# A Mamba layer between two sparse FFNs on one core: paired scans, the inverse root in PSUM, one gate instruction, moved ticks

## The reference, cut to what matters

```python
def ffn(x):                                    # H = 512, I = 2048
    h = silu(x @ w_gate) * (x @ w_up)
    return keep_two_largest_of_each_four(h) @ w_down
def mam(x):                                    # E = 1024, N = 16, DT = 128
    xn = x * rsqrt(mean(x*x) + EPS) * norm_w
    skip, u = xn @ W_skip.T, silu(conv4(xn @ W_in.T) + conv_b)
    delta = softplus(u @ Wd1.T @ Wd2.T + bd2)
    Bt, Ct = u @ WB.T, u @ WC.T
    h = exp(delta[..., None] * A) * h + (delta * u)[..., None] * Bt    # scan over time
    y = sum_n(h * Ct)
    return ((y + u * W_D) * silu(skip)) @ W_out.T
```

## Time and profile before

| | |
|---|---|
| three runs | 3527.07, 3531.05, 3532.09 us; median 3531.05 |
| the profiled execution | 3525.57 us |
| its span, first to last instruction | 3523.6 us |
| mean granted TensorE clock | 0.987 of 2.4 GHz |
| PE busy | 3339.9 us |
| DVE busy | 3031.5 us |
| POOL busy | 2597.2 us |
| ACT busy | 1999.2 us |
| DMA | 696.44 MB, mean 198 GB/s |

### The profile page before, as it was taken

The page is one execution under the profiler, slowest core; times in us unless marked ns, Lnnn a source line. Parts: engine busy times, 40 slices in busy tenths (PEclk is TensorE's granted clock), DMA queues, the critical chain, the costliest instruction groups (busy, mean ns, idle before and its releaser), DMA issues. The chain is left out here.

```text
span 3523.6 us, 39028 instructions
## 1 busy us (share of the span) xinstructions
PE 3339.9 (95%) x12020; PEld 2110.5 (60%) x12020; DVE 3031.5 (86%) x3597; ACT 1999.2 (57%) x2760; POOL 2597.2 (74%) x1625
## 2 busy tenths in 40 slices
PE   8999999999999999999999999999879889998899
PEld 6775656556655665556655665556545555555467
DVE  5546998789999889989998999999989998999934
ACT  5545656557565664557565674656555665454422
POOL 1315876667878778778787788878989888989913
PEclk9999999999999999999999999999999999999999
DMA  9656566656656566467665675647645565656433
GB/s 362 220 188 195 175 212 219 216 177 222 216 180 227 187 222 227 153 203 230 185 216 185 199 241 179 207 164 237 222 127 206 173 204 211 185 158 196 136 125 117
DMA packets 243469, 696.44 MB, mean 198 GB/s; under 512 B 23536, under 2 KB 23792, under 8 KB 233584
## 3 DMA queue, kind: packets, MB, share of 16 engines
q1 hardware_dynamic: 173632, 559.72, 45.6%
q10 hardware_dynamic: 69632, 134.23, 14.5%
HBM read 619.94 MB, written 76.55 MB: 198 GB/s over the span
## 5 line engine op out<-in xcount | busy, mean ns | idle before, releaser
L1439 POOL TENSOR_TENSOR scan_in<-du,scan_rows 128x512 f32<-128x512 f32 x1024 | 1317.1, 1302 | 628.2 <-DVE decay L1313 537.0
L1313 DVE TENSOR_TENSOR_SCAN decay<-decay,scan_in 128x512 f32<-128x512 f32 x1024 | 1250.8, 1221 | 23.8 <-ACT decay L915 16.5
L1452 POOL TENSOR_TENSOR y<-y,scan_out 128x1024 f32<-128x1024 f32 x512 | 1227.3, 2397 | 0.6 <-DVE scan_out L1323 0.6
L915 ACT ACTIVATE decay<-delta,small 128x512 f32<-128x512 f32 x1024 | 696.9, 688 | 905.4 <-DVE scan_out L1323 897.5
L684 PE MATMUL side<-zhi,wunit 128*128 128x512 f32 x2048 | 905.6, 442 | 40.2 <-DVE zlo L1217 22.5
L774 PE MATMUL side<-h,wdown 128*128 128x512 f32 x1760 | 799.7, 598 | 23.5 <-DVE res_g L1298 12.7
L686 PE MATMUL side<-zhi,wunit 128*128 128x512 f32 x2048 | 814.4, 398 | 0.0
L685 PE MATMUL side<-zlo,wunit 128*128 128x512 f32 x2048 | 812.6, 397 | 0.0
L1323 DVE TENSOR_TENSOR scan_out<-decay,scan_rows 128x512 f32<-128x512 f32 x1024 | 702.6, 686 | 33.3 <-POOL y L1452 8.2
L774 PEld LDWEIGHTS side<-h,wdown 128*128 128x128 f32 x1760 | 333.2, 191 | 391.8 <-issue 347.7
L902 ACT ACT_TABLE_LOAD x407 | 522.2, 1283 | 7.2
(11 more groups left out here) (109 smaller groups left out, 2890.4 us busy)
## 6 DMA issues: line engine op xcount, KB each, us to landing
wunit<-hl_dram SPq DMA_DIRECT2D x480, 512.0 KB, 4.3
scan_rows<-bc_dram ACTq DMA_DIRECT2D x256, 512.0 KB, 5.7
wdown<-down_w_dram SPq DMA_DIRECT2D x256, 256.0 KB, 3.1
wmam<-mam_dram SPq DMA_DIRECT2D x128, 512.0 KB, 4.2
hl_dram<-wunit SPq DMA_DIRECT2D x32, 512.0 KB, 5.2
skip_dram<-skb SPq DMA_DIRECT2D x64, 256.0 KB, 4.6
delta<-skip_dram SPq DMA_DIRECT2D x16, 1024.0 KB, 7.2
wmam<-wout_dram SPq DMA_DIRECT2D x32, 512.0 KB, 4.4
```

The costliest lines, as they stand in the source:

```text
L915: nc.scalar.activation(decay[u % BANKS][:], delta[:, e, :], ACT.Exp, scale=aneg[:, e * N + n:e * N + n + 1]).then_inc(sem["decay_ready"], 1)
L1313: nc.vector.tensor_tensor_scan(decay[u % BANKS][:], decay[u % BANKS][:], db[u % INPUTS][:], 0.0, ALU.mult, ALU.add).then_inc(sem["state_re ...
L1439: nc.gpsimd.tensor_tensor(db[u % INPUTS][:], du[:, e, :], rows[m % ROWS][:, 0, :], ALU.mult).then_inc(sem["input_ready"], 1)
L1452: nc.gpsimd.tensor_tensor(y[:, e:e + 2, :], y[:, e:e + 2, :], scan_out[:, k:k + 2, :], ALU.add).then_inc(sem["sum_ready"], 1)
```

## The change

- DVE's `begin` does two scans and then the two products with C, where a quarter has two units or more.
- The inverse root is written back into the bank that held the variance, and `scale` reads it there (L1203, L1208, L1211). The bank's next owner waits for `scaled`; the planner counts it as taken one tick longer (1.9). The Ln's result stays in SBUF, under a semaphore of its own.
- `gate` is one instruction of 128x2048 in place of four.
- The late deltas go to `STARTS[b] + 7` and `+ 8`. STARTS, and with it all that hangs on it (gates, output projections, some norms and projections), goes from (67, 130, 190, 250, 310, 363, 409, 454, 516) to (67, 130, 191, 250, 312, 359, 409, 454, 515). The pause of seven ticks ahead of product 47 stands ahead of product 45. From its second tick on a half has at least three units done.
- ACT loads a batch's first rows only when its `fold` is past, and takes no unit ahead of time whose delta isn't.
- The planner's costs become tables at the head of the file, with the same values except `var`.

```diff
-PAUSES = {0: 9, 34: 1, 47: 7, 224: 4, 384: 1, 416: 1, 448: 4, 480: 24}
+PAUSES = {0: 9, 34: 1, 45: 7, 224: 4, 384: 1, 416: 1, 448: 4, 480: 24}
...
-STARTS = (67, 130, 190, 250, 310, 363, 409, 454, 516)
+STARTS = (67, 130, 191, 250, 312, 359, 409, 454, 515)
...
-                self.jobs_at[STARTS[b] + 8 + e // 2].append(("dl", b, HE + e))
+                self.jobs_at[STARTS[b] + 7 + e // 2].append(("dl", b, HE + e))
...
-                    upto = start + min(HALF, int(total + 0.5)) if t < end - 1 else start + HALF
+                    upto = start + min(HALF, max(int(total + 0.5), 3 * (t > first))) if t < end - 1 else start + HALF
...
-        read = {"win": 0.2, "down": 0.25, "out": 0.25, "mean": 0.3, "msum": 0.1, "vsum": 0.1, "in": 0.9, "var": 0.9}
+READ = {"win": 0.2, "down": 0.25, "out": 0.25, "mean": 0.3, "msum": 0.1, "vsum": 0.1, "in": 0.9, "var": 1.9, ...
...
         def wait_read(eng, key):
-            eng.wait_ge(sem[f"side_read_{plan.bank_of[key]}"], plan.turn_of[key])
+            if key[0] == "var":
+                eng.wait_ge(sem["scaled"], key[1] + 1)
+            else:
+                eng.wait_ge(sem[f"side_read_{plan.bank_of[key]}"], plan.turn_of[key])
...
                 if u % HE == BANKS - 1:
-                    load_rows(u // HE + 2)
+                    due.append(u // HE + 2)
+                    load_due()
+            def load_due():
+                while due and (due[0] >= B * GROUPS or now[0] > plan.tick_of_job["fold", due[0] // GROUPS] + 1):
+                    load_rows(due.pop(0))
...
                 for u in range(units_done[0], max(units_done[0], min(end + EXP_LEAD, B * UNITS) if end else 0)):
+                    b, half = divmod(u // HALF, 2)
+                    if u >= end and now[0] <= plan.tick_of_job["dl", b, HE * half + HE - 1] + 1:
+                        return
                     unit(u)
...
-                                     scale=1.0 + EPS if double else 1.0).then_inc(read_of(key), 1)
-                wait_read(act, key)
-                nc.scalar.activation(rs, rt, ACT.Exp, scale=-0.5).then_inc(sem["root_ready"], 1)
+                                     scale=1.0 + EPS if double else 1.0).then_inc(sem["log_ready"], 1)
+                act.wait_ge(sem["log_ready"], i + 1)
+                nc.scalar.activation(bank_of(key)[:], rt, ACT.Exp, scale=-0.5).then_inc(sem["root_ready"], 1)
...
                 dve.wait_ge(sem["root_ready"], i + 1)
+                rs = bank_of(("var", i))[:]
...
                 for u in units:
-                    if u > units.start:
+                    second = (u - units.start) % 2
+                    if u > units.start and not second:
                         times_c(u - 1)
                     scan(u)
+                    if second:
+                        times_c(u - 1)
...
-                for k in range(HE):
-                    e = HE * half + k
-                    nc.vector.tensor_tensor(y[:, e, :], y[:, e, :], delta[:, gates_in(b, half).start + k, :],
-                                            ALU.mult).then_inc(sem["gated_ready"], 1)
+                es = halves[half]
+                nc.vector.tensor_tensor(y[:, es, :], y[:, es, :], delta[:, gates_in(b, half), :], ALU.mult).then_inc(sem["gated_ready"], HE)
```

More of the change, by code:

```diff
@@ L85 @@
 SPLIT_AT = 10
+VECTOR = {"mean": 2.3, "down": 0.3, "out": 0.7, "win": 0.6, "in": 1.1, "up": 0.7, "step": 2.9, "low": 2.0, "scale": 3.0, "gate": 2.2, "du": 3.0, "unit": 1.99}
+TENSOR = {"dt": 6.9, "bc": 1.8, "fold": 1.2, "msum": 0.9, "mean": 0.6, "vsum": 0.9, "var": 0.9, "dl": 0.0, "win": 0.7, "down": 3.5, "in": 3.5, "skip": 3.5,
+          "out": 3.5, "product": 2.8}
+READ = {"win": 0.2, "down": 0.25, "out": 0.25, "mean": 0.3, "msum": 0.1, "vsum": 0.1, "in": 0.9, "var": 1.9, "skip": 0.6, "dt": 0.6, "bc": 0.6, "fold": 0.6, "dl": 0.6,
+        "gate": 0.35, "up": 1.35, "first up": 0.55}
 EXP_TABLE, SILU_TABLE, SOFTPLUS_TABLE = "natural_log_exp_and_others", "silu_and_others", "softplus"
@@ L194, in place_units @@
     def place_units(self):
-        vector = {"mean": 2.3, "down": 0.3, "out": 0.7, "win": 0.6, "in": 1.1}
-        tensor = {"dt": 6.9, "bc": 1.8, "fold": 1.2, "msum": 0.9, "mean": 0.6, "vsum": 0.9, "var": 0.9, "dl": 0.0, "win": 0.7}
-        unit = 1.99
+        vector, tensor, unit = VECTOR, TENSOR, VECTOR["unit"]
         def other(tick):
@@ L203, in other @@
             if self.product_at[tick - 1] is not None and is_up(self.product_at[tick - 1]):
[L204 to L207, removed]
+                cost += vector["up"]
+            cost += vector["step"] * (tick - 2 in self.base)
+            cost += vector["low"] * (tick in self.ffn_start or tick in self.split_x_at) + vector["scale"] * (tick in self.scale_at)
+            return cost + vector["gate"] * (tick in self.gate_at) + vector["du"] * (tick in self.du_at)
         def work(tick):
-            return 2.8 * (self.product_at[tick] is not None) + sum(tensor.get(key[0], 3.5) for key in self.jobs_at[tick])
+            return tensor["product"] * (self.product_at[tick] is not None) + sum(tensor[key[0]] for key in self.jobs_at[tick])
         self.units_at = [range(0)] * self.ticks
@@ L242, in place_banks @@
                 if not is_up(n):
-                    free = self.tick_of[4 * (n // 4) + 1] + 1.35
+                    free = self.tick_of[4 * (n // 4) + 1] + 1 + READ["gate"]
                 else:
-                    free = tick + (2.35 if j else 1.55)
+                    free = tick + 1 + READ["up" if j else "first up"]
                 product = [(("product", n), free)]
@@ L248, in place_banks @@
             for key in jobs:
-                side.append((key, tick + 1 + read.get(key[0], 0.6)))
+                side.append((key, tick + 1 + READ[key[0]]))
                 if key[0] == "var" and key[1] in self.alone:
@@ L261, in place_banks @@
                 owner[k] = key
-            if key[0] not in ("awake", "product"):
+            if key[0] not in ("awake", "product", "var"):
                 turns[k] += 1
@@ L362, in build @@
         sq = sb("sq", [P, KD, L])
-        parts, rt, rs = sq[:, 0, :], sq[:, 1, :], sq[:, 2, :]
+        parts, rt = sq[:, 0, :], sq[:, 1, :]
         dts = sb("dts", [P, L])
@@ L382, in build @@
             "member_high_ready", "member_split_ready", "down_high_ready", "down_split_ready",
-            "centred_tile", "squared_tile", "scaled_tile", "squares_ready", "quarter_ready", "root_ready", "scaled", "high_part_ready", "normed_ready",
+            "centred_tile", "squared_tile", "scaled_tile", "squares_ready", "quarter_ready", "log_ready", "root_ready", "scaled", "high_part_ready", "normed_ready",
             "decay_ready", "input_ready", "state_ready", "weighted_ready", "sum_ready",
@@ L916, in unit @@
                 if u % HE == BANKS - 1:
-                    load_rows(u // HE + 2)
+                    due.append(u // HE + 2)
+                    load_due()
+            due, now = [], [0]
+            def load_due():
+                while due and (due[0] >= B * GROUPS or now[0] > plan.tick_of_job["fold", due[0] // GROUPS] + 1):
+                    load_rows(due.pop(0))
             def upto(end):
                 for u in range(units_done[0], max(units_done[0], min(end + EXP_LEAD, B * UNITS) if end else 0)):
+                    b, half = divmod(u // HALF, 2)
+                    if u >= end and now[0] <= plan.tick_of_job["dl", b, HE * half + HE - 1] + 1:
+                        return
                     unit(u)
@@ L1125, in _ @@
                 jobs = plan.jobs_at[tick - 1] if tick else []
+                now[0] = tick
+                load_due()
                 if tick == plan.norm_m[0]:
```

## The result

The changed kernel takes 3488.97 us (median of four runs, 3484.88 to 3490.21) against 3530.86 for the kernel before in the same comparison (four runs, 3527.07 to 3532.09): a ratio of 0.9884, interval 0.9872 to 0.9895, or 41 us. The prediction, 3517.6 in a range of 3499 to 3537, had the sign right and a third of the size, and the range does not hold the result. The profiled execution has a span of 3486.3 us at a mean granted clock of 0.988, against 3523.6 and 0.987 before: 37 us.

The account below looks back on a forecast made before the run. PE was taken to bound two thirds, DVE and PE in turn the last third, POOL close behind. Terms -9.9 -1.5 +0.5 -4 +4.4 -2.5 +1 +2 -3.4 gave -13.4 us: 3531.05 to 3517.6, range 3499 to 3537.

Parts of the forecast that it names:

- Root: Norm scales on DVE stop waiting for POOL with the inverse root in PSUM: -9.9 us for L1211, -1.5 for L1203.
- the wait is not removed: Rival: the output or first input delays L1211, so the root's gain and most of the clock's go: 3531 us, chance 0.08.
- Bank held longer: The variance's bank stays taken until DVE's scale ends, so its next owner may wait: +0.5 us, ends 0 and +8.
- Gate: Four gate pieces in one: -4 us from DVE, +4.4 from PE's later first piece, ends -8 and +8 together.
- Pairs: Two scans, then two products on DVE in quarters with two or more units: -2.5 us, ends 0 and -6.
- Guards: ACT's limits on row loads and early exponentials never hold anything back in the new ticks: 0 us.
- PE's banks only, 0 +-2: Late deltas one tick earlier would affect only PE's banks: 0 us, give or take 2.
- STARTS: Moved batch starts shift DVE and PE load between half batches, batch 5's counting most: +2 us, ends -12 and +20.
- More is given back: Rival: all DVE time saved in the last third becomes PE's and the clock recovers: 30 us, 3501, chance 0.18.
- POOL took over: Rival: in the last three halves saved DVE time only idles before POOL: about -7 us, 3524, chance 0.12.
- The slower case: Rival: batch 4's second half becomes bound by DVE, batch 5's stays at 1.29: 3541 us, chance 0.12.
- Clock: PE's granted clock recovers 0.31 us per us of idle time given back, 11 us in all: -3.4 us.

Follow-up runs that it names:

- late_only: Kernel before with only the late deltas one tick earlier in all eight batches: 3511.98 us, ratio 0.9951.
- s359_only: Kernel before with only batch 5's start at tick 359 in place of 363: 3528.36 us, ratio 0.9993.
- s312_only: Kernel before with only batch 4's start at tick 312 in place of 310: 3528.52 us, ratio 0.9996.
- ticks_only: Kernel before with the whole new plan alone (STARTS, pause, late delta, three units from a half's second tick): 3503.28 us, ratio 0.9929.
- after_best: Changed kernel with second-half gates of batches 2, 6 and 7 in four pieces and batch 5's start at 360: 3477.53 us, ratio 0.9852.
- pair_only: Kernel before with only the order of two scans, then two products: 3524.97 us, ratio 0.9991.

## Why the prediction was right in sign and wrong in size

1. *Root: right, and in its term's bounds.* -11.4 and its part of the clock (0.31 of that, 3.5) make -15; measured -17 alone, 12 to 22. The instruction's wait is gone as computed, in all fourteen. One reading in it was too small: "only a few waited" of the 32 pieces L1203, but their mean was 881 ns against a median of 744, 4.4 us of waits, and DVE got 4.6 back. The rule beside it is in the Trainium skill, "SBUF — State Buffer", section "Who interferes with whom": a DVE instruction with two SBUF inputs contends with a GpSimd one that reads SBUF, one with at most one SBUF input does not. The trace agrees: 2.276 to 2.282 us with one, up to 4.986 for the gate, which keeps two. The longer PSUM source time that the prediction cited does not show: 2.278 against the 2.284 of the earlier trace rows. The rival "the wait is not removed" is refuted.
2. *Bank held longer: nothing seen.* In the trace after, no wait of PE is ended by DVE's scale (L1223, L1228 or L1231), which now frees the bank.
3. *Gate: the term was mis-sized,* 0.4 for a measured -8 alone. Its two halves were near (-7.8 us of DVE, PE's first piece 1.6 us late), the first by a slip: a third of 14.3 is 4.8 and not 4.3. I let half of DVE's time count; by the balance it counted whole or more, and up to 6 us of the 8 go with the clock.
4. *Pairs:* -2.5 forecast, 3 measured. *Guards:* the two never hold anything back in the plan; not run alone.
5. *The step that failed is the late delta, "PE's banks only, 0 +-2".* It measured -17 (13 to 22) alone. The banks were named and then not priced, and they were not the only thing: I did not list the jobs of the ticks that the deltas leave and enter, nor look at PE's line in them, where the waits stood to be read: 0.98 and 1.95 us for banks in `STARTS[4] + 9` of before, and 4.39 us for weights in `STARTS[3] + 7`. I had priced a move of work by its amount, which did not change; its cost lies in what else stands in the tick. The windows of these two batches hold 7 of the 12 us that late_only's windows gain; the rest is in batches 2, 5, 6 and 7, and its waits were not read.
6. *STARTS:* the signs and sizes by half were right (169.6, 196.3, 175.4 against 176, 197, 178) and the net near nothing, as s359_only and s312_only show. The late delta (-17) and these two (-2.5 and -1.4) make 21 of the plan's 25 us; the pause, the third and the ninth start and the floor of three units hold the rest, within the uncertainty, and were not separated. One place of it is seen: PE's wait for weights in `STARTS[3] + 7`, 2.24 us in late_only, is gone in ticks_only, where their load lands 4.1 us after its issue.
7. *Rivals.* "More is given back" named the right direction but not the place: it looked to the last third, while half of the gain lies before. POOL took over nowhere: the halves at 2250.8 and 2447.1 stay above its 154 us by 42 and 21. In the last half it is close: 161.2 us in place of 163.6, POOL busy 151.2 of them (94%). The slower case did not come: batch 4's second half took 169.6, far from 185.
8. *Clock: the rate held, the idle time was too small.* In the two profiles PE idles 29 us less and is busy 8 less, 0.27 us per us, near the 0.31; but the sum had 11 us of idle time (its items 1, 3 and 4 add up to 13.5, so even by itself it should have had 4.2 in place of 3.4). By the runs' clocks the term is at most 17 to 19 us, against 3.4.

With -17 in place of 0 and -8 in place of +0.4 the sum would be -39 us. That this is near the 41 measured is luck: it keeps +3 for the rest of the plan, where the parts measured about -8, and leaves out the 12 us by which the parts overlap.

## What to carry to other kernels

Before a side job is moved by a tick, list what else wants a bank or ACT's turn in its old and its new tick, and what load the next job needs, and read PE's waits in both: the same work one tick earlier gave 0.5% here, and crowded into one tick it cost 0.2%. A DVE instruction that read two SBUF tiles beside a busy POOL got its shortest time back here (2.28 us in all fourteen) when one operand was left in PSUM. Merging instructions saves their waits, but keep the pieces where the consumer stands ready for the first.

## What the runs showed of the hardware

The granted clock makes single profiles of nearly the same kernel scatter. A stretch that late_only changes little (products 64 to 96), before and in late_only:

```profile
389.53:596.60 207.07, 202.03 (x756) 133.04 (x757) 193.08 (x233) 125.51 (x169) 158.02 (x98) 0.99 0.66 207
```

```profile
390.47:594.45 203.98, 199.95 (x753) 131.95 (x757) 192.62 (x233) 125.34 (x169) 157.82 (x98) 1.00 0.68 211
```

The one with a short time at half speed takes 3.1 us longer. In all, the profiles spent between 76 us (after_best) and 131 us (s312_only) of their spans at the lower of the two levels, before 92 and pair_only 123. So a gain is read here from the rounds; a difference of a few us between two traces says where to look and no more, unless an idle time or a tick shows it. And the DMA that brings a projection's weights (512 KB) landed 7.1 us after its issue in one place before (PE idled 4.39 us for it at 1555.97), 6.6 in late_only, and 4.1 in ticks_only, with no idle time: a load issued just ahead of its use is a cost that no table of work holds, and here it stood in a tick of two jobs.
